# A masked attention whose mask product serves a chain of four heads instead of two

## The reference, cut to what matters

```
def _L0_xattn_ref(X, encoder_output, causal_mask, padding_mask, ...):
    B, LQ, LKV = (4, 256, 256)
    HID, H, G = (512, 32, 8)            # 32 heads of 16 in 8 key groups
    q = X @ Wq.T + bq                   # -> b, G, 4, 256, 16
    k = encoder_output @ Wk.T + bk      # -> b, G, 256, 16
    v = encoder_output @ Wv.T + bv
    scores = jnp.einsum('bgrqd,bgkd->bgrqk', q, k) / jnp.sqrt(jnp.float32(HD))
    scores = jnp.where(causal_mask[None, None, None, :, :], -jnp.inf, scores)
    scores = jnp.where(padding_mask[:, None, None, None, :], -jnp.inf, scores)
    w = jax.nn.softmax(scores, axis=-1)
    out = jnp.einsum('bgrqk,bgkd->bgrqd', w, v)
    ...
    return out @ Wo.T + bo
```

## Time and profile before

| | |
|---|---|
| median of 3 runs | 1681.04 us (1680.8 to 1686.86) |
| profiled execution | 1678.48 us, span 1676.7 us |
| PE busy | 1579.1 us (94% of the span) |
| DVE, ACT, POOL busy | 974.4, 710.3, 824.1 us |
| granted TensorE clock, mean | 0.984 of full |
| first attention, eight bodies | 75.9 to about 492 us of the span |

### The profile page before, as it was taken

The page is one execution under the profiler, slowest core; times in us unless marked ns, Lnnn a source line. Parts: engine busy times, 40 slices in busy tenths (PEclk is TensorE's granted clock), DMA queues, the critical chain, the costliest instruction groups (busy, mean ns, idle before and its releaser), DMA issues. The chain is left out here.

```text
span 1676.7 us, 29168 instructions
## 1 busy us (share of the span) xinstructions
PE 1579.1 (94%) x10826; PEld 827.4 (49%) x10826; DVE 974.4 (58%) x1947; ACT 710.3 (42%) x1311; POOL 824.1 (49%) x853
## 2 busy tenths in 40 slices
PE   5889999999889999899999989999999999999998
PEld 3456666565544444345556544444444444444443
DVE  5756676778748999835655543377564333322246
ACT  3288887888885556523232221211111111133321
POOL 3488887877864445433543434344342442022234
PEclk9899999999799999999999999999999999999999
DMA  7764544323344554434454426455553755287856
GB/s 187 170 124 100 112 99 114 90 62 74 92 96 94 120 123 104 91 79 89 98 120 91 79 71 162 101 122 132 98 123 79 151 123 107 77 191 190 191 146 193
DMA packets 453955, 195.66 MB, mean 117 GB/s; under 512 B 395501, under 2 KB 418287, under 8 KB 453817
## 3 DMA queue, kind: packets, MB, share of 16 engines
q1 hardware_dynamic: 448136, 175.19, 46.8%
q0 software_dynamic: 5680, 18.62, 4.4%
HBM read 77.17 MB, written 22.81 MB: 60 GB/s over the span
## 5 line engine op out<-in xcount | busy, mean ns | idle before, releaser
L1143 POOL TENSOR_TENSOR a_pl<-a_prob,a_ph 128x512 f16<-128x512 f32 x256 | 295.4, 1167 | 73.9 <-ACT a_prob L1032 73.3
L1232 DVE TENSOR_REDUCE a_mx<-bank 128x2 f32<-128x512 f32 x256 | 173.1, 686 | 86.8 <-PE bank L730 85.1
L140 PE MATMUL bank<-XTh,d_whs 128*128 128x512 f16 x512 | 194.7, 380 | 3.8 <-PEq L89 2.4
L141 PE MATMUL bank<-XTl,d_whs 128*128 128x512 f16 x512 | 194.8, 380 | 0.0
L142 PE MATMUL bank<-XTh,d_wls 128*128 128x512 f16 x512 | 194.8, 380 | 0.0
L1031 ACT ACTIVATE a_ph<-bank 128x512 f16<-128x512 f32 x256 | 153.8, 601 | 59.7 <-PE bank L750 33.0
L2434 POOL CAST d_cut<-d_raw 128x512 f16<-128x512 f32 x90 | 55.8, 620 | 227.8 <-DMA d_raw<-in_L_ffn_sw 146.0
L1032 ACT ACTIVATE a_prob<-bank 128x512 f32<-128x512 f32 x256 | 154.2, 603 | 0.0
L2354 DVE TENSOR_TENSOR d_hid<-d_hid,bank 128x512 f32<-128x512 f32 x64 | 43.9, 686 | 168.0 <-PE bank L142 164.1
L2345 ACT ACTIVATE d_hid<-bank 128x512 f32<-128x512 f32 x64 | 38.2, 597 | 204.7 <-PE bank L142 204.7
L2349 ACT ACTIVATE d_hh<-d_hid 128x512 f16<-128x512 f32 x64 | 40.3, 629 | 193.3 <-DVE d_hid L2354 193.3
(11 more groups left out here) (348 smaller groups left out, 3994.3 us busy)
## 6 DMA issues: line engine op xcount, KB each, us to landing
d_raw<-in_L_ffn_w SPq DMA_DIRECT2D x48, 256.0 KB, 3.0
d_raw<-in_L_ffn_sw SPq DMA_DIRECT2D x42, 256.0 KB, 3.1
made<-e_y SPq DMA_DIRECT2D x39, 256.0 KB
a_stage<-in_L_ffn_w_fc SPq DMA_DIRECT2D x32, 256.0 KB, 2.9
a_stage<-in_L_ffn_w_proj SPq DMA_DIRECT2D x32, 256.0 KB, 3.1
a_fbuf<-in_ctx SPq DMA_DIRECT2D x16, 256.0 KB, 3.2
rows<-f_cut SPq DMA_DIRECT2D x16, 256.0 KB, 2.4
out_x<-X SPq DMA_DIRECT2D x16, 256.0 KB, 2.4
```

Source lines behind the costliest of these rows:

```text
L140: nc.tensor.matmul(out_ap, lhi, rhi, start=first, stop=False)
L141: nc.tensor.matmul(out_ap, lhi, rlo, start=False, stop=False)
L1143: nc.gpsimd.tensor_tensor(pl[:, n % NP, :], prob[:, n % 2, :], ph[:, n % NP, :], ALU.subtract).then_inc(ev["L"], 1)
L1232: nc.vector.tensor_reduce(mx[:, h, tt, half, 2 * (g % 4):2 * (g % 4) + 2], bank[BS + m % 2][:, :].rearrange("p (r k) -> p r k", r=2), AX_X ...
```

## The change

What it does, in order:
- **Chain of four.** `which` gives each step a bank (`m % 2`), a half and a place j of 8. Both products of a step belong to two key groups, g and g + 4 (r = 0, 1), and four steps of one bank go through the four heads of each. After the first head come three differences, so the query chunks needed are heads (0,1), (1,2), (2,3) of a group: `query_chunk` picks among 30 chunks. The mask product comes in steps 0 and 1 of every eight (`m % 8 < 2`), in `scores` and `turned_scores`. `turned_scores` now has two products of 256 with their own key chunks in place of one of 512.
- **Queries.** `place_q` writes the pairs and the pairs shifted by one head: 8 DMA transposes for a half, of 4 chunks each, but the shifted ones of half 1 of 3. `place_maxima` writes with 3 DMAs.
- **First queries.** Batch 0's first half is turned by `turn_q` and taken by DVE as before. Batch 0's second half and batch 1's first are turned by `turn_early` on PE into banks `BAV` and copied by ACT (`take_early`). `place_q(1, 0)` is gone from SP.
- **Rest.** The maxima's order in `mx` follows. `normalise` multiplies in two parts of half the size. `on` has one buffer instead of two, and waits for `To1` of the batch before. `brow` and `blow` lie in its space. `WO_AT` is (3, 7, 12, 16). Three chain semaphores become one. `turn_k` takes groups in the new order, `times_v` too.

```diff
--- before.py
+++ after.py
@@ -456,7 +459,7 @@
     CUT_AT = [1, 6, 11, 17, 23, 28]
-    WO_AT = [12, 14, 16, 18]
+    WO_AT = [3, 7, 12, 16]
     LAST_AT = [1, 3, 5, 7, 9, 11, 13, 15, 17, 19, 21, 23, 25, 27]
...
@@ -469,8 +472,18 @@
-        u = m % 16
-        return u // 8, 4 * (m // 16) + 2 * (u // 4 % 2) + u % 2, u // 2 % 2
+        return m % 2, m // 16, m // 2 % 8
+
+    def key_chunk(h, r, j):
+
+        first = j == 0 or j == 4
+        return 8 * h + 4 * r + 2 * (j // 4) + (0 if first else 1)
+
+    def query_chunk(h, r, j):
+
+        if j % 2:
+            return 16 * h + j - 1 + r
+        return 16 * h + j + r if j % 4 == 0 else 16 * h + 8 + j - 2 + r
...
@@ -544,20 +557,25 @@
             sp.wait_ge(ev["nc"], 2 * b + h + 1)
-            for half in range(2):
-                r = 4 * HD0 * half + NEG
-                sp.dma_start(qT[r:r + 1, b % 2, 8 * h:8 * h + 8, :], nT[8 * half:8 * half + 8, h, :])\
-                  .then_inc(ev[f"ng{h}"], 16)
+            first, second = NEG, 4 * HD0 + NEG
+            to = 16 * h
+            sp.dma_start(qT[first:first + 1, b % 2, to:to + 14, :], nT[0:14, h, :]).then_inc(ev[f"ng{h}"], 16)
+            sp.dma_start(qT[second:second + 1, b % 2, to:to + 8, :], nT[8:16, h, :]).then_inc(ev[f"ng{h}"], 16)
+            sp.dma_start(qT[second:second + 1, b % 2, to + 8:to + 14, :], nT[2:8, h, :]).then_inc(ev[f"ng{h}"], 16)
...
                 sp.wait_ge(ev[f"lq{tt}"], b + 1)
-                for u in range(2):
-                    p0 = 8 * h + 4 * u
-                    sp.dma_start_transpose(qT[:, b % 2, p0:p0 + 4, tt * P:(tt + 1) * P],
-                                           qs[:, tt, 2 * p0:2 * p0 + 8, :].rearrange("p h c -> p (h c)"))\
+                for r in range(2):
+                    h0, to = 8 * h + 16 * r, 16 * h + r
+                    sp.dma_start_transpose(qT[:, b % 2, to:to + 7:2, tt * P:(tt + 1) * P],
+                                           qs[:, tt, h0:h0 + 8, :].rearrange("p h c -> p (h c)"))\
+                      .then_inc(ev[f"tq{h}"], 16)
+                    n = 3 if h else 4
+                    sp.dma_start_transpose(qT[:, b % 2, to + 8:to + 7 + 2 * n:2, tt * P:(tt + 1) * P],
+                                           qs[:, tt, h0 + 1:h0 + 1 + 2 * n, :].rearrange("p h c -> p (h c)"))\
                       .then_inc(ev[f"tq{h}"], 16)
...
@@ -601,7 +619,6 @@
             load_piece(l)
-        place_q(1, 0)
         place_maxima(0, 0)
...
@@ -688,18 +705,27 @@
-        def turn_q(b, tt, h):
-            if h == 0 and tt == 0:
-                wait("lq0", b)
-                wait("lq1", b)
-                if b:
-                    wait("nc", b - 1, 1, 2)
+        def turn_q(tt, i):
+            if i == 0 and tt == 0:
+                wait("lq0", 0)
+                wait("lq1", 0)
             else:
-                wait("cq", b, 2 * h + tt, 4)
+                pe.wait_ge(ev["cq"], 2 * i + tt)
             for j in range(8):
-                c = qs[:, tt, 16 * h + 2 * j:16 * h + 2 * j + 2, :].rearrange("p h c -> p (h c)")
+                h0 = 16 * (j % 2) + 2 * (j // 2) + i
+                c = qs[:, tt, h0:h0 + 2, :].rearrange("p h c -> p (h c)")
                 last = nc.tensor.transpose(bank16(BM)[:, j * P:(j + 1) * P], c, ident16[:, :])
             last.then_inc(ev["tq"], 1)
+
+        def turn_early(b, h, tt, i):
+            n = 4 * b + 2 * i + tt
+            if n >= 2:
+                pe.wait_ge(ev["cm"], n - 1)
+            for j in range(6 if h and i else 8):
+                h0 = 16 * (j % 2) + 2 * (j // 2) + i + 8 * h
+                c = qs[:, tt, h0:h0 + 2, :].rearrange("p h c -> p (h c)")
+                last = nc.tensor.transpose(bank16(BAV + n % 2)[:, j * P:(j + 1) * P], c, ident16[:, :])
+            last.then_inc(ev["tm"], 1)
...
@@ -739,28 +768,31 @@
         def turned_scores(b, par, n):
-            g, half, kc = n // 4, n // 2 % 2, n % 2
-            bk = bank[BST + n % 2]
+            kc, h, j = which(n)
+            bk = bank[BST + kc]
             wait("E", b, n + 1, NS)
             if n % 16 == 0:
-                wait(f"ng{n // 16}", b, 32, 32)
-            if half == 0:
+                pe.wait_ge(ev[f"ng{h}"], 48 * (b + 1))
+            if n % 8 < 2:
                 nc.tensor.matmul(bk[:, :].rearrange("p (r k) -> p r k", r=2), ident16[:, :],
                                  maddT[:, kc, :].unsqueeze(1).broadcast_to([P, 2, S]), start=True, stop=True)
-            nc.tensor.matmul(bk[:, :], kT[:, par, 2 * g + half, kc * P:(kc + 1) * P],
-                             qT[:, par, 2 * g:2 * g + 2, :].rearrange("p r q -> p (r q)"),
-                             start=False, stop=True, skip_group_check=True).then_inc(ev["ST"], 1)
+            for r in range(2):
+                last = nc.tensor.matmul(bk[:, r * S:(r + 1) * S], kT[:, par, key_chunk(h, r, j), kc * P:(kc + 1) * P],
+                                        qT[:, par, query_chunk(h, r, j), :], start=False, stop=True,
+                                        skip_group_check=True)
+            last.then_inc(ev["ST"], 1)
...
-            g, half, kc = n // 4, n // 2 % 2, n % 2
+            p, j, kc = n // 8, n // 2 % 4, n % 2
             if n % 8 == 0:
-                wait("ON", b, g // 2 + 1, G0 // 2)
+                wait("ON", b, p + 1, G0 // 2)
             wait("L", b, n + 3, NS)
-            into = bank[BAV + g // 2 % 2]
+            into = bank[BAV + p % 2]
             for r in range(2):
+                g = p + 4 * r
                 for qt in range(2):
-                    c = (((qt * 2 + g % 2) * 2 + r) * 2 + half) * (HD0 + 1)
+                    c = ((qt * 2 + r) * 4 + j) * (HD0 + 1)
                     q = slice((2 * r + qt) * P, (2 * r + qt + 1) * P)
...
@@ -843,8 +875,9 @@
             for tt in range(2):
-                turn_q(0, tt, h)
+                turn_q(tt, h)
                 turn_k(0, tt, h)
+                turn_early(0, 1, tt, h)
         for m in range(NS):
...
@@ -853,6 +886,8 @@
                 turn_maxima(0, 0)
+            if 18 <= m < 22:
+                turn_early(1, 0, m % 2, (m - 18) // 2)
             if m in (22, 26):
...
@@ -927,10 +962,14 @@
             if b >= 2:
-                act.wait_ge(ev["tq0"], 64 * (b - 1))
-                act.wait_ge(ev["tq1"], 64 * (b - 1))
+                if b == 2:
+                    act.wait_ge(ev["tm"], 8)
+                else:
+                    act.wait_ge(ev["tq0"], 128 * (b - 2))
+                act.wait_ge(ev["tq1"], 128 * (b - 1))
             elif b:
                 wait("tq", 0, tt + 3)
+                act.wait_ge(ev["tm"], tt + 3)
             nc.scalar.activation(qs[:, tt, :, 0:2 * HD0].rearrange("p h (r c) -> p h r c", r=2),
...
@@ -950,10 +989,18 @@
+        def take_early(b, h, tt, i):
+            n = 4 * b + 2 * i + tt
+            act.wait_ge(ev["tm"], n + 1)
+            c, k = 16 * h + 8 * i, 6 if h and i else 8
+            nc.scalar.activation(qT[:, b, c:c + k, tt * P:(tt + 1) * P],
+                                 bank16(BAV + n % 2)[:, 0:k * P].rearrange("p (j q) -> p j q", j=k),
+                                 ACT.Copy).then_inc(ev["cm"], 1)
+
         def take_maxima(b, h):
...
             if b:
-                act.wait_ge(ev[f"ng{h}"], 32 * b)
+                act.wait_ge(ev[f"ng{h}"], 48 * b)
             nc.scalar.activation(nT[:, h, :], bank16(BM)[0:H0 // 2, 0:2 * P], ACT.Copy).then_inc(ev["nc"], 1)
...
@@ -1015,10 +1062,16 @@
         high_kv(0, 1)
+        for i in range(2):
+            for tt in range(2):
+                take_early(0, 1, tt, i)
         for tt in range(2):
...
         take_maxima(0, 0)
+        for i in range(2):
+            for tt in range(2):
+                take_early(1, 0, tt, i)
         normal(2, 0)
...
@@ -1226,10 +1279,10 @@
         def maxima(b, m):
-            tt, g, half = which(m)
-            h = m // 16
+            tt, h, j = which(m)
+            e = 8 * (j % 2) + 2 * (j // 2)
             wait("S", b, m + 1, NS)
-            nc.vector.tensor_reduce(mx[:, h, tt, half, 2 * (g % 4):2 * (g % 4) + 2],
+            nc.vector.tensor_reduce(mx[:, h, tt, e:e + 2],
                                     bank[BS + m % 2][:, :].rearrange("p (r k) -> p r k", r=2), AX_X, ALU.max)\
...
@@ -1246,12 +1299,15 @@
             link(nc.vector.reciprocal(rec[:, p % 2], o[:, :, :, HD0]))
-            if b >= 2 and p == 0:
-                wait("To1", b - 2)
-            nc.vector.tensor_tensor(on[:, b % 2, :, p * P:(p + 1) * P].rearrange("p t (h c) -> p t h c", h=8),
-                                    o[:, :, :, 0:HD0],
-                                    rec[:, p % 2].unsqueeze(3).broadcast_to([P, 2, 8, HD0]), ALU.mult)\
-              .then_inc(ev["ON"], 1)
+            if b and p == 0:
+                wait("To1", b - 1)
+            for r in range(2):
+                g = p + 4 * r
+                last = nc.vector.tensor_tensor(
```

(14 more changed lines are left out.)

46 lines of the change are left out of this document (25 added, 21 removed).

## The result

The changed kernel takes 1717.9 us in the median of 4 runs (1714.2 to 1718.3), the kernel before 1681.0 (4 runs, 1680.8 to 1686.9). The ratio is 1.0215, with a 95% interval of 1.0194 to 1.0235: 36.9 us slower, where I had said 24; it lies inside my range of 1688 to 1721, near its upper end. The profiled execution took 1714.2 us, with a span of 1712.4 and a mean granted clock of 0.966. The span of before was 1676.7, so its own account must explain +35.7 us where my sum had +26.3.

A forecast was written before the change was run, and what follows sets the result against it. PE, busy 94% of the span, was taken as the bound, with SyncE's queue at the critical path's edge. Terms summed to +26.3 us: 1704.8 on the profiled 1678.5, 1707 by the median, stated as 1705; range 1688 to 1721.

The forecast's parts named there:

- What decides: SyncE's queue at the starts of bodies 1 to 6: maxima stand behind 8 transposes instead of 4, and PE waits.
- +4 to +6: The forecast case, chance 0.70: each of the six starts of bodies 1 to 6 comes 4 to 6 us later.
- The run of eight: At starts of bodies 1 to 6: 8 transposes at 1.28 us, maxima 2.0, landing 1.6; 13.9 us to the first product.
- How much of the mask saving arrives: PE in each body: of 3.45 us a batch saved, 1.7 reach step 25 and 1.9 the body's end.
- The clock: Behind each start the clock falls: 1.2 us more in bodies 1, 2, 3, 5 and 6, 0.4 in body 4.
- Bodies 1 to 5: Periods against the old ones: +5.6, +5.1, +3.7, +3.9 and +3.8 us.
- Body 0: Queue freer before step 26, `place_q(2, 0)` at some 118.6 instead of 119.96: -1.35 + (13.9 - 8.47) = +4.1 us.
- The rest of the longer queue hides.: `place_maxima(b, 1)` and `place_q(b+1, 1)` end 13 and 11 us into the body, wanted at step 16; weight loads are ahead.
- Bodies 6 and 7: No `place_q(b+2, 0)` in body 6; cold start +1.2, masks -1.0 and -0.5: -0.3 us together.
- The queue keeps up: Rival, chance 0.06: transposes shorter or maxima early enough, so PE's gain counts: -12 us, about 1668.
- partly covered: Rival: the wait at the starts comes partly covered, 1691 us; with 8 transposes in 8.5 us, 1681, chance 0.07.
- The DMA engines fall behind: Rival, chance 0.17: transposes take 1.6 us each, +2.6 at each of 6 starts, +15.4, about 1720 us.

The follow-up runs named there:

- the two kernels with masks: Removed mask products put back in the relieved kernel (1693.0 us, ratio 1.0084) and in the one with earlier projections (1689.4 us, ratio 1.0045).
- the kernel kept at work: Changed kernel plus 15 to 29 extra mask products on PE ahead of the wait for the maxima, bodies 1 to 6: 1715.8 us, ratio 1.0200.
- relieved kernel with masks: Relieved kernel with a second mask product in steps 4 and 5 of every eight, in `scores` and `turned_scores`: 1693.0 us, ratio 1.0084.
- relieved kernel: Changed kernel with `place_out` 0 to 2 ahead of body 0, `place_x` halved at steps 18 and 22, `place_q(b+2, 0)` at 20 and 26: 1687.9 us, ratio 1.0038.
- earlier projections: Relieved kernel with the query projections of batch b+2 three steps earlier (PQ from (15, 21) to (12, 18)): 1684.3 us, ratio 1.0024.

## Why the prediction was right, and where its sum was not

- *What decides.* Right. The queue, read last, was the view that mattered: the kernel before with a longer queue alone gives 1.0225. That the time fell inside my range has luck in it: three of the six starts came later by more than the "+4 to +6" that I had given each (+11.8, +6.8, +6.6; the others +5.4, +6.0, +3.9), the loss was half as large again as I had said, and the upper end of the range, which covers it, came from a rival that was wrong.
- *The run of eight.* I had 13.9 us from first transpose to first product; it was 14.4, 13.9, 14.8, 14.6, 14.6 and 14.2. I had divided the 5.12 us of the earlier trace rows by four; from one to the next are 1.31 us, and in most of the runs one took 0.3 to 0.8 us longer. Landing was 1.20 us each time, less than my 1.6. The two errors partly cancel: +3.1 us in six starts.
- *How much of the mask saving arrives.* I said 1.7 us by step 25. With the clock held up, first product to `place_q` was 1.0, 1.7, 0.6 and 1.6 us under that of before in bodies 1, 2, 3 and 5 (42.94 against 43.91, and so on): 1.2 in the mean. Where I let the waits for DVE swallow a part, they swallowed more: in body 1 the wait for `a_v` was 1.5 us instead of 1.1, and small ones for `a_nT` (0.4) and `a_qs` (0.3) were new. In whole kernels the masks were worth 5.1 us by the medians (7.7 and 3.5 by the ratios), not 15. I had looked only for waits that would swallow them. By the estimates beside the two kernels with masks, the lower clock of the kernels without them took 10 to 13.5 us of the saving, a term that I had put at nothing.
- *The clock.* I took 1.2 us per start. The clock fell at all six, to 0.50 to 0.63 over the first 4 us, and the kernel kept at work shows 1.3 us for four bodies. The rule of the Trainium skill ("TensorE: Matmul & The Clock Gate", section "HAM oscillation — how this bites in real kernels") that each turn of a loop which waits for a DMA begins at the low clock holds here, by these windows. But of the six falls' cost at most some 2 us stand in the whole time, and these are not clear of the noise. My "Without the fall the sum below would be 6.4 us lower" is not what the run shows.
- *Bodies 1 to 5.* The sum of these terms was 22.1; measured 28.6. The mask term (+0.5 a body), the run (+0.5 a body) and, in body 4, the clock, to which I had given only 0.4, make most of it.
- *Body 0: the step that failed.* "so the queue is freer before step 26, though `place_q(1, 1)` in step 0 grows by 5.1. Then I take `place_q(2, 0)` to be bound by step 25, at some 118.6" instead of 119.96. It began at 125.89. I weighed the two edits only at the end of the body. Both stand ahead of `place_ctx(3)`, and GpSimd's `x_high` waits for that one. From the body's first product to `place_q(2, 0)` were 49.9 us, where my step had 42.7: 7.2 us of the 9.4 that the sum lacked. Taking the two `place_out` away from there gave 5.3 back in the trace. The other 1.9 are the gain of 1.35 us that I had put there, which did not come (44.6 us without the two, 44.1 before).
- *"The rest of the longer queue hides."* Right for `place_maxima(b, 1)` and the loads, and for step 16, which had no wait. I did not name `place_ctx`, which stands behind `place_q(b+1, 1)` too, and so missed the one thing that was not hidden. In bodies 1 to 4 it did hide: GpSimd waited 1.4, 0.6, 1.4 and 1.2 us, against 0.9 to 1.4 in bodies 0 to 3 of before.
- *Bodies 6 and 7.* -2.3 instead of -0.3. Most of it is body 6 (48.93 against 50.78), although its clock was at 0.63 over the first 4 us, as foreseen. What shortened it is not shown.
- *The rivals.* "The queue keeps up" and "partly covered" needed shorter runs, and runs were longer. "The DMA engines fall behind" gave 1720, close to what was measured, and for the wrong reason: the pace stayed at 1.31 us, not 1.6. That the sum of that rival hits the time is chance.

## What to carry to other kernels

A queue that issues in order has as many deadlines in a loop's body as there are kinds of transfer in it. Before adding to it, list for each transfer behind the new ones who waits for it and with what slack in the trace; a wait of 0.9 us on an engine off the critical path is a deadline already met late. When a full queue is the bound, moving an item earlier only pays if it goes into a stretch in which the queue stood, and work saved on the engine that was the bound before is worth little: here 27.6 us of products gave 3.5 to 7.7. Part of such a saving turns into waits, and on PE a further part into time at the lower clock, so read the granted clock of both kernels beside their waits.

## What was not expected of the hardware

- A transpose of 128 x 512 f16 takes its queue 1.31 us from one to the next, whether its destination is four neighbouring chunks, every second chunk (`L573`, `L577`) or a tile of its own. In most runs of eight one took longer, up to 2.9 us (299.10 in the kernel whose PE was kept at work).
- The landing took 1.20 us behind the last of the maxima, to within 0.02 us at all six starts, although eight transposes stood ahead of them.
- PE's clock was low behind each of the six waits, the shortest of which was 3.57 us. Behind shorter ones it went either way: over the next 4 us it was 0.57 after waits of 1.94 us (relieved kernel with masks, 183.46) and 2.66 us (relieved kernel, 239.31), and 1.00 after waits of 2.00 us (with masks, 130.06) and 2.19 us (earlier projections, 233.12).
